# Half projections as two 64-row passes beside the scores, and a new order inside the slots

## The reference

```
q = norm(x) @ Wq + bq                 # 16 heads of 16
k = ctx @ Wk + bk ; v = ctx @ Wv + bv # 4096 keys for each of 4 batches
out = softmax(q k^T / 4) v            # for each batch and head
```

## Time and profile before

| | |
|---|---|
| Median of 3 runs | 1417.14 us (1416.73 to 1419.59) |
| The profiled execution's own time | 1416.92 us |
| Its span, first to last instruction | 1415.1 us |
| Mean granted TensorE clock | 0.986 |
| PE busy / PEld / DVE / ACT / POOL | 1357.3 / 793.4 / 1071.3 / 960.0 / 287.2 us |
| First scores, last scores | 65.2 us, 947.1 us |

### The profile page before, as it was taken

The page is one execution under the profiler, slowest core; times in us unless marked ns, Lnnn a source line. Parts: engine busy times, 40 slices in busy tenths (PEclk is TensorE's granted clock), DMA queues, the critical chain, the costliest instruction groups (busy, mean ns, idle before and its releaser), DMA issues.

```text
span 1415.1 us, 32674 instructions
## 1 busy us (share of the span) xinstructions
PE 1357.3 (96%) x13282; PEld 793.4 (56%) x13282; DVE 1071.3 (76%) x2114; ACT 960.0 (68%) x1997; POOL 287.2 (20%) x321
## 2 busy tenths in 40 slices
PE   7799999999999999999999999899999999989998
PEld 4244555444555444555444545457557999856666
DVE  4777787888787888787888888725876768767757
ACT  5367787877788777888777666753796654348731
POOL 3344222212212222212223000000003100001110
PEclk9799999999999999999999999998999999999999
DMA  6846454345454345454345522001402320356000
GB/s 177 190 135 160 118 138 110 75 115 137 107 139 111 71 119 137 105 138 114 70 109 160 131 46 46 2 15 47 120 24 64 110 66 1 93 122 147 1 1 30
DMA packets 98791, 134.55 MB, mean 95 GB/s; under 512 B 11024, under 2 KB 74128, under 8 KB 92688
## 3 DMA queue, kind: packets, MB, share of 16 engines
q1 hardware_dynamic: 98640, 132.45, 37.4%
HBM read 94.15 MB, written 38.27 MB: 94 GB/s over the span
## 4 chain that ended last, share of the span: by engine, by line
PE 86%; DVE 7%; ACT 5%; issue 1%; DMA 1%; SPq 0%; POOL 0%; ACTq 0%; DVEq 0%; POOLq 0%
PE psum L553 19%; PE psum L573 17%; PE psum L534 7%; PE psum L606 4%; PE psum L2182 4%; PE psum L2156 3%; PE psum L653 3%; PE psum L1276 2%; PE psum L2901 2%; DVE peaks L714 2%; ACT probs L812 2%; PE psum L613 2%; PE psum L1673 1%; PE psum L275 1%; PE psum L2911 1%; PE psum L2864 1%
## 5 line engine op out<-in xcount | busy, mean ns | idle before, releaser
L714 DVE TENSOR_REDUCE peaks<-psum 128x1 f32<-128x512 f32 x1024 | 656.1, 686 | 157.5 <-PE psum L534 147.7
L812 ACT ACTIVATE probs<-psum 128x512 f32<-128x512 f32 x1024 | 556.3, 596 | 181.0 <-PE psum L553 170.2
L553 PE MATMUL psum<-queriesT,keysT 64*128 64x256 bf16 (+1 forms) x4096 | 332.6, 274 | 16.6 <-ACT probs L812 16.1
L553 PEld LDWEIGHTS psum<-queriesT,keysT 64*128 64x128 bf16 (+1 forms) x4096 | 166.3, 95 | 210.7 <-ACT probs L812 167.2
L573 PE MATMUL psum<-probs,values 128*17 128x256 f32 x4096 | 271.7, 383 | 0.0
L534 PE MATMUL psum<-keysT,queriesT 64*128 64x512 bf16 x1024 | 211.1, 381 | 8.6 <-DMA keysT<-key_parts 4.9
L573 PEld LDWEIGHTS psum<-probs,values 128*17 128x17 f32 x4096 | 94.2, 96 | 128.0 <-issue 77.8
L962 POOL CAST key_parts<-key_f 128x512 bf16<-128x512 f32 x57 | 34.7, 609 | 494.9 <-ACT key_f L851 452.0
L534 PEld LDWEIGHTS psum<-keysT,queriesT 64*128 64x128 bf16 x1024 | 59.9, 95 | 31.5 <-DVE peaks L714 18.9
L606 PE MATMUL psum<-ctxT,wk 128*128 128x256 f32 x192 | 67.1, 431 | 0.2 <-DVE peaks L714 0.2
L968 POOL TENSOR_TENSOR key_parts<-key_r,key_parts 128x512 bf16<-128x512 f32 x57 | 65.9, 1157 | 4.6
(11 more groups left out here) (321 smaller groups left out, 1739.3 us busy)
## 6 DMA issues: line engine op xcount, KB each, us to landing
keysT<-key_parts SPq DMA_DIRECT2D x186, 256.0 KB, 5.8
key_parts<-key_parts SPq DMA_DIRECT2D x90, 256.0 KB
ctx_nat<-in_ctx_dram SPq DMA_DIRECT2D x32, 256.0 KB, 3.2
ctx_in<-in_ctx_dram SPq DMA_DIRECT2D x24, 256.0 KB, 4.7
ctx_turned<-ctxT SPq DMA_DIRECT2D x24, 256.0 KB, 6.2
ctx_T<-ctx_turned SPq DMA_DIRECT2D x12, 512.0 KB, 4.0
qk_parts<-early_weights SPq DMA_DIRECT2D x24, 128.0 KB
q_parts<-q_parts SPq DMA_DIRECT2D x20, 128.0 KB
```

Source lines behind the costliest of these rows:

```text
L553: made = e.matmul(ps[j][:, e2 * S:(e2 + 1) * S], self.keysT[own, plane, i % RING, kt * P:(kt + 1) * P], self.queriesT[own, plane, u % 2, g ...
L714: e.tensor_reduce(self.peaks[:, i % 2, j * QT + qt, c:c + 1], k.ps(("max", n)), AX.X, ALU.max).then_inc(*self.peaked.up(n))
L812: e.activation(self.probs[:, t % RINGP, 2 * j * S:(2 * j + 2) * S], k.ps(("scores", t, j)), ACT.Exp).then_inc(*self.exped.up((t, j)))
```

## The change

- A half projection, of keys or of values, is cut into two float32 matmuls of 64 rows: part 0 on rows 0 to 63, part 1 on rows 64 to 127. Part 1 adds to part 0 in the same bank and waits for its end (a new semaphore, `half_made`).
- An even slot with a half issues: part 0; the four score matmuls of head j=1; the two maxima; the first two score matmuls of j=0; part 1; the last two of j=0. An even slot without a half issues its scores alternately and then the maxima, as before.
- An odd slot with maxima mixes them with the scores, both halves of the rows getting the same work; then the weighing, then the jobs. Without maxima the scores are alternate.
- The two heads are called early and late: (1, 0) in even slots and (0, 1) in odd ones. Score banks and exponentials follow that order, and VectorE takes the two maxima of an odd slot in reverse.
- `make values` for b>0 is gone: each is two `make half` two slots apart. There are now 192 halves in 192 even slots. `turn ctx` moves from even slots to odd ones and `normalize` too; `turn x` and `make queries` move from odd to even ones and come every 4 slots instead of every 6. Loads, turns and saves of the context come 15 to 16 slots earlier, with waits by chunk instead of by batch.

```diff
-SCORES, SUMS, BLOCK = (0, 1, 2), 3, 2
+HALVES, SUMS, BLOCK = 3, 3, 2
+HALF_JOBS = "fill half", "make half"
+def order(t):
+    return (0, 1) if t % 2 else (1, 0)
...
         for b in range(1, B):
-            at(6 * b, "norm x", b)
-            at(6 * b + 3, "scale x", b)
-            at(6 * b + 5, "turn x", b)
-            at(6 * b + 7, "make queries", b)
-            at(6 * b + 10, "write queries", b)
+            at(4 * b - 2, "norm x", b)
+            at(4 * b, "scale x", b)
+            at(4 * b + 2, "turn x", b)
+            at(4 * b + 4, "make queries", b)
+            at(4 * b + 8, "write queries", b)
...
-                    at(slot - 15, "load ctx", b, c)
-                    at(slot, "turn ctx", b, c)
-                    at(slot + 6, "save ctx", b, c)
+                    at(slot - 31, "load ctx", b, c)
+                    at(slot - 15, "turn ctx", b, c)
+                    at(slot - 10, "save ctx", b, c)
...
-                at(SLOTS * i + SLOTS + 4, "normalize", i)
+                at(SLOTS * i + SLOTS + 5, "normalize", i)
...
             for b in range(1, B):
-                slot = SLOTS * NG * b
-                if p in self.HALF_VALUES:
-                    for e2, after in enumerate(self.HALF_VALUES[p]):
-                        at(slot + after, "make half", b, p, e2)
-                else:
-                    at(slot - 94 + 8 * p, "make values", b, p)
+                for e2 in range(2):
+                    at(SLOTS * NG * b - 110 + 8 * p + 2 * e2, "make half", b, p, e2)
...
+        def score(t, j, *steps):
+            i, p = divmod(t, SLOTS)
+            u, g = divmod(i, UNIT_GROUPS)
+            if steps[0] == 0:
+                banks.use((2 * t + order(t).index(j)) % HALVES, w, ("scores", t, j), (self.exped, (t, j)))
+            ps = k.ps(("scores", t, j))
+            for step in steps:
+                e2, plane = divmod(step, 2)
...
+        def half_job(t, part, job, *a):
+            own = slice(part * HALF, (part + 1) * HALF)
...
+            if part == 0:
+                misc(t, name, (kept, done))
+                w.wait_ge(*self.ctx_turned(b, c))
+                e.matmul(k.ps(name)[:, 0:S], stationary, moving, start=True, stop=False).then_inc(
+                    *self.half_made.up((job,) + tuple(a)))
+            else:
+                w.wait_ge(self.half_made, (job,) + tuple(a))
+                e.matmul(k.ps(name)[:, 0:S], stationary, moving, start=False, stop=True).then_inc(*made_by.up(done))
...
+            half, = halves
+            early, late = order(t)
+            half_job(t, 0, *half)
+            score(t, early, 0, 1, 2, 3)
             for n in maxima:
                 find_max(n, t)
+            score(t, late, 0, 1)
+            half_job(t, 1, *half)
+            score(t, late, 2, 3)
+
+        def odd_slot(t, maxima):
+            early, late = order(t)
+            if not maxima:
+                both_scores(t)
+                return
+            first = maxima[0]
+            score(t, early, 0)
+            find_max(first + late, t)
+            score(t, early, 1, 2)
+            score(t, late, 0)
+            score(t, early, 3)
+            score(t, late, 1)
+            find_max(first + early, t)
+            score(t, late, 2, 3)
...
-                for j in range(GH):
+                for j in order(t):
                     w.wait_ge(self.scored[j], (t, j))
```

More of the change, by code:

```diff
@@ L463, in plan @@
         at(STREAM_STARTS[1] + 32, "stream", "next turn", 0)
+        for jobs in due.values():
+            jobs.sort(key=lambda job: job[0] not in HALF_JOBS)
         return due
@@ new lines, in both_scores @@
+        def both_scores(t):
+            early, late = order(t)
+            for step in range(4):
+                score(t, early, step)
+                score(t, late, step)
+        def half_job(t, part, job, *a):
+            own = slice(part * HALF, (part + 1) * HALF)
+            if job == "fill half":
+                u, c, h = a
+                b, m = divmod(u, KD)
+                name, done = ("keys", u, c, h), (u, c) if h else ("half", u, c)
+                kept, made_by = self.key_kept, self.key_made
+                at, stationary = c * BANK + h * S, self.wk[own, 0, m * P:(m + 1) * P]
+                moving = self.ctxT[own, at:at + S]
+            else:
+                b, p, e2 = a
+                c, at = 2 * p * P // BANK, (2 * p + e2) * P
+                name, done = ("v", b, p, e2), (b, p) if e2 else ("half", b, p)
+                kept, made_by = self.v_kept, self.v_made
+                stationary, moving = self.ctxT[own, at:at + P], self.wv[own, 0, :]
+            if part == 0:
[3 more added lines that the diff above has]
+                    *self.half_made.up((job,) + tuple(a)))
+            else:
+                w.wait_ge(self.half_made, (job,) + tuple(a))
+                e.matmul(k.ps(name)[:, 0:S], stationary, moving, start=False, stop=True).then_inc(*made_by.up(done))
@@ new lines, in weigh @@
+        def weigh(t):
+            if not BLOCK + 1 <= t <= TOTAL + 1:
+                return
+            i, p0 = divmod(t - BLOCK - 1, SLOTS)
+            b, g = divmod(i, NG)
+            w.wait_ge(self.exped, (t - 2, order(t)[1]))
+            for p in range(p0, p0 + BLOCK):
+                w.wait_ge(self.v_kept, (b, p))
+            w.wait_ge(self.ones_set, b % 2)
+            if i:
+                w.wait_ge(self.outT_kept, i - 1)
+            w.wait_ge(self.cleared, 0)
+            for p in range(p0, p0 + BLOCK):
+                for e2 in range(2):
+                    for j in range(GH):
+                        quad, half, kt = e2 * GH + j, 2 * j + e2, 2 * p + e2
+                        made = e.matmul(k.bank(SUMS)[32 * quad:32 * quad + DH + 1, 0:S],
+                                        self.values[b % 2][:, kt, g * GH + j, :],
+                                        self.probs[:, (SLOTS * i + p) % RINGP, half * S:(half + 1) * S],
+                                        start=(p == 0), stop=(p == SLOTS - 1))
+            made.then_inc(*self.weighed.up((t - BLOCK - 1) // BLOCK))
@@ new lines, in even_slot @@
+        def even_slot(t, maxima):
+            halves = [job for job in self.due.get(t, ()) if job[0] in HALF_JOBS]
+            w.wait_ge(self.shiftT_kept, t // SLOTS)
+            w.wait_ge(self.ones_in, 0)
+            if not halves:
+                both_scores(t)
+                for n in maxima:
+                    find_max(n, t)
+                return
+            half, = halves
+            early, late = order(t)
+            half_job(t, 0, *half)
+            score(t, early, 0, 1, 2, 3)
@@ L557, in tensor @@
             for n in maxima:
                 find_max(n, t)
[L559 to L577, removed]
@@ L579, in tensor, with jobs @@
+        def jobs(t):
             for job, *a in self.due.get(t, ()):
@@ L657, in tensor @@
                     k.stream.tensor_job(e, w, lambda job, *let_go: misc(t, job, *let_go), *a)
+        for t in range(FIRST, TOTAL + 3):
+            maxima = self.maxima(t)
+            if t < 0 or t >= TOTAL:
+                for n in maxima:
+                    find_max(n, t)
+                if t % 2:
+                    weigh(t)
+                jobs(t)
+            elif t % 2:
+                odd_slot(t, maxima)
+                weigh(t)
+                jobs(t)
+            else:
+                even_slot(t, maxima)
+                jobs(t)
         banks.let_go[SUMS] = [(self.outT_kept, GROUPS - 1)]
@@ L728, in peak, with jobs @@
                 *self.shift_found.up(("rest", i)))
-        for t in range(FIRST, TOTAL + 3):
-            for n in self.maxima(t):
-                peak(n)
+        def jobs(t):
             for job, *a in self.due.get(t, ()):
@@ L771, in vector @@
                     k.stream.vector_job(e, w, *a)
+        for t in range(FIRST, TOTAL + 3):
+            made = self.maxima(t)
+            for n in reversed(made) if 0 <= t < TOTAL and t % 2 else made:
+                peak(n)
+            jobs(t)
     def scale_heads(self, e, w, i):
@@ L798, in scalar, with exponentials @@
         k = self.k
-        for t in range(FIRST, TOTAL + 3):
+        def exponentials(t):
             if 0 <= t < TOTAL:
@@ L903, in scalar @@
                     k.stream.scalar_job(e, w, *a)
+        for t in range(FIRST, TOTAL + 3):
+            exponentials(t)
+            keep_sums(t)
+            jobs(t)
     def pool_chunks(self):
@@ L948, in gpsimd @@
                     inverse(QT * a[0])
-                elif job == "make values" and a == [1, 0]:
+                elif job == "make half" and a == [1, 0, 0]:
                     w.wait_ge(self.q_made, B - 1)
```

56 lines of the change are left out of this document (19 added, 37 removed).

## The result

The change makes the kernel **8.9% slower**: 1541.92 us in the median of four runs (1540.4 to 1546.64) against 1416.93 of the kernel before (four runs, 1415.45 to 1419.59), a ratio of 1.0885 with a 95% interval of 1.0856 to 1.0915. Forecast were 1401 us in a range of 1366 to 1428. The profiled execution took 1540.4 us, its span is 1538.6. The kernel was rewritten around the changed part, so its lines are others: scores L551, maxima L537, weighing L605, part 0 and part 1 of a half L582 and L586, VectorE's reduction L786, the exponential L891, ScalarE's copies of a half of keys L936 and of values L946.

A forecast was written before the change was run, and what follows sets the result against it. TensorE's sequence of starts was taken as the bound (86% of the chain). Terms -12.2, +2.2, -2.2, +1.0, -1.7 and -3.0 sum to -15.9 us, from 1416.9 to 1401 us, range 1366 to 1428.

The forecast's parts named there:

- Costed at nothing: ScalarE and VectorE: Slot pairs: four exponentials at 1.96 us plus about 0.8 for copies fit under 3.04, so neither engine adds time.
- Rival 4: The gain goes into waits (late ScalarE, query chain, maxima banks): some 10 us given back, 1411 us or no change; chance 0.14.
- The even slot: Even slot with a half: rows 0 to 63 free at 1.205 us, rows 64 to 127 at 1.285; pair 3.04 against 3.16.
- The halves' term: All key and value halves on TensorE: 129.3 us before, 117.1 after for 192 of them, so -12.2 us.
- `turn shift`: 24 times behind a half in even slots: one more change of the array's form each, on 0.21 us before; +2.2 us.
- `turn ctx` in the odd slot: 24 times behind the weighing instead of between 64-row passes: one change of the array's form less, -2.2 us.
- Empty even slots: 22 later even slots with maxima but no job: pair 2.90 for 3.12, -4.8; six moved `normalize` +1.8; together -3.0 us.
- The middle: The long middle stretch of the slots, 129 to 767 us before, should shrink by some 11 us.
- Slots 0 to 32: Query jobs fill waits behind empty even slots, against a later query chain (+2.6) and denser VectorE norms (+1): -1.7 us.
- strict program order: Passes start strictly in order, even across row halves: even slot with a half about 1.42 us, total 1427 us; chance 0.14.
- Hidden loads: Weight loads of the half's parts go under neighbouring passes: even slot 1.10 to 1.15 us, total 1366 us; chance 0.17.
- types that can't share: Float32 and bf16 passes can't share the array, every switch drains: even slot 2.47 us, total 1629 us; chance 0.05.

The follow-up runs named there:

- experiment 5: The changed kernel, but an odd slot's maximum whose turn falls on the PSUM bank of the half just made takes the next bank: 1397.18 us.
- experiment 8: The kernel of experiment 5, but each batch's query parts are written two slots earlier in SyncE's order: 1395.73 us.

## Why the prediction was wrong

**The step that failed** is the paragraph "Costed at nothing: ScalarE and VectorE". It checked ScalarE's throughput (1.96 + 0.8 under 3.04, which holds) and the rotation of the three banks of the scores. The other rotation, banks 4 to 7, was never laid out: who takes a bank four places behind the half, when it is due, and when ScalarE has copied the half. All of that was in the code and in the earlier trace rows. Rival 4 named the place, "maxima banks", and gave it "some 10 us"; it was the mis-sized term. In slots 32 to 413 the changed kernel loses against that of experiment 5, from start to start in the two traces (mean us of a pair of slots):

| pairs | number | changed | experiment 5 | loss |
|---|---|---|---|---|
| half of keys | 72 | 3.858 | 3.048 | 58.3 us |
| half of values | 59 | 3.767 | 3.033 | 43.3 |
| half and `turn shift` | 23 | 4.298 | 3.615 | 15.7 |
| half, odd slot with `turn ctx` or `normalize` | 33 | 4.33 to 4.72 | 3.59 to 3.98 | 24.3 |

In all 141.6 us; the two middle stretches differ by 141.8 (761.6 and 619.8), and slots 0 to 32 by 2.3 more. Of the profiled executions, the change without the wait gains 20.9 us (1416.9 to 1396.0) and the wait takes 144.4 (1396.0 to 1540.4): together the 123.5 us between the profiled executions of before and after.

**The other steps** can be read in the kernel of experiment 5, whose profiled execution took 1396.0 us against a forecast of 1401, and in the changed kernel itself:

- *The even slot*: forecast 1.285 on rows 64 to 127 and 1.205 on rows 0 to 63; measured 1.29 and 1.19. Part 1 after 0.75: right. Early scores within 0.02: 0.01. The pair: 3.04 forecast, 3.04 measured (3.03 with a half of values, 3.05 with one of keys, in the mean). The halves' term, -12.2, comes out as -13.1 against the forecast's own 129.3: a half costs 0.605 us (1.188 + 1.848 - 0.675 - 1.756), 192 of them 116.2. The 129.3 were a little too few, though: by the mean pairs of each kind in the two traces (keys 3.184 before and 3.048 now, one half of values 3.154 and 3.033, two of them 3.585) the halves gave back some 15.7 us.
- *`turn shift`*: forecast +2.2, measured +4.7. It costs 0.579 us now (3.615 - 3.036) and cost 0.373 before (3.527 - 3.154), not 0.21: in the old kernel the odd slot behind it was 0.16 longer, which the even slot's start-to-start time in the earlier trace rows does not show.
- *`turn ctx` in the odd slot*: 0.587, and 0.68 in the even slot before (1.355 - 0.675), one change of form less as forecast. *`normalize`* alone costs 0.555 there (forecast 0.45 + 0.11).
- *Empty even slots*: the pair is 2.90 as forecast. But the stretch from slot 416 on shrank by 1.5 us (1.2 in experiment 5), not by 3. Pair by pair against experiment 5, fifteen pairs there give back 0.22 each (3.3 us) where nineteen were forecast; the pairs that `normalize` moved into lose 1.5 (forecast 1.8), and pairs with a `turn shift` or with jobs of the later stages lose another 0.7, which the forecast left out.
- *The middle* shrank by 18.2 us (638.0 to 619.8), where some 11 were forecast. A part is work moved ahead: four halves and two `turn ctx` now stand before slot 32. Another was not priced: between slots 32 and 411 nine even slots had neither a half nor a `turn ctx` before, in pairs of 3.09 where two slots without a wait take 2.43 (0.675 + 1.756); now there are three. From the first to the last scores it is 863.5 us for 882.0, that is -18.5 for a forecast of -15.9; so the total came out near by errors of both signs, too.
- *Slots 0 to 32*: GpSimd's split of the second batch's queries began at 100.44 (forecast 100.6). ScalarE waited for it 4.8 us (forecast 2.6). The slots took 0.9 us more in experiment 5 than before (64.7 for 63.8) instead of 1.7 less. The wait itself went in experiment 8.
- *Later stages*: "don't change", but from the last scores to the end it is 468.0 us before, 465.3 in experiment 5 and 469.0 in experiment 8, with the same program. The granted clock was 0.98, 0.99 and 0.97 in these stretches, so the differences fit the clock rather than the change; 2.7 us of them are in the 5 between 1396 and 1401.

So the gain of the two passes was argued rightly and nearly to size, and only the kernel without the bank wait shows it. Of the rivals, strict program order (1427) had the right side for a wrong reason: the starts 0.01 apart exclude it. Hidden loads (1366) and types that can't share (1629) are excluded by the same rows. The last line of the prediction said it would be wrong if TensorE showed new idle time before the scores on ScalarE in slots with a half. The idle time came before the maxima of the slot behind.

The Trainium skill's rule on strict order of starts ("TensorE: Matmul & The Clock Gate", section "The mechanism") does not hold for the second pass of a float32 matmul: in the timeline of the changed kernel the second pass of part 0 starts at 588.42, while scores issued behind it have been starting since 588.11.

## What to carry to other kernels

Moving a user to another place of a rotation changes which two users share a bank, even where the number of banks and the work stay the same: write down the period (users, banks, who is k places ahead) and for each shared pair two times, when the later user is due and when the reader of the earlier one has finished, with the reader's own order. An engine that is far from full can still hold the bound one if what is waited for stands second in its queue. And price a job by the whole period that contains it, not by its own slot, since part of its cost shows in the slot behind.

## What the runs showed of the hardware

- **A float32 pass on rows 0 to 63 runs beside bf16 passes on rows 64 to 127 at no visible cost.** The four early scores of an even slot end at 588.72 (588.45 + 0.27), 0.61 after their start at 588.11; a row of eight alternate scores lasts 0.62. No row of the kernel before had shown the two types together.
- **The end of a bf16 score beside a float32 pass seems to be told late.** In the timeline above ScalarE starts on it 0.17 us after its modelled end (588.89 against 588.72). In the even slots from 32 to 398 the first exponential of the kernel before starts about 0.10 after that end in 138 of 184 cases and 0.03 to 0.04 after it in 46; in the changed kernel, whose slots there all hold a half, it is about 0.23 in 137 and 0.17 in 46. That is 0.13 later. The float32 pass issued ahead of the score ends at 588.80 (588.42 + 0.38), 0.08 after the score. Ends that are told in program order, while starts are not, would fit the direction, but account for 0.08 of the 0.13. No run isolates this; it stays open. ScalarE's chain starts later by it, and TensorE stands for 1 us in 620 in experiment 5 all the same.
- **A wait for one half of the rows holds the other half too.** In the changed kernel the second maximum (at 590.55) waits, and the scores on the other rows behind it in the queue start at 590.56, although they need nothing that it waits for. Part 1's own wait had been costed that way, and there it is free; here both halves stand still for one.
